# Edge scores of a graph attention layer on one core: a buffer of its own for the 49th bin's rows, a ring of four leaky results, three lane buffers, and the small work of a pair spread over its steps

## The reference, cut to what matters

```python
hij = jnp.concatenate([h[src], h[dst]], axis=-1)
e = jnp.matmul(jax.nn.leaky_relu(jnp.matmul(hij, w), 0.2), a)
exp_e = jnp.exp(e)
denom = jax.ops.segment_sum(exp_e, src, num_segments=N)
```

## Time and profile before

| | us |
|---|---|
| median of 3 runs | 3370.88 |
| lowest and highest run | 3368.73, 3375.42 |
| the profiled execution | 3371.61 |
| its span, first to last instruction | 3369.8 |
| DVE busy in the span | 3095.1 (92%) |
| PE busy / PEld busy | 3073.6 (91%) / 2791.6 (83%) |
| ACT busy | 2725.8 (81%) |

### The profile page before, as it was taken

How to read it: one execution, slowest core, us unless ns; L and a number is a source line. 1 busy time by engine, 2 the same in 40 slices (tenths; PEclk the granted TensorE clock), 3 DMA queues, 4 the chain that set the end, 5 groups by cost and what they waited for, 6 DMA issues and landing times. The chain is left out here.

```text
span 3369.8 us, 100973 instructions
## 1 busy us (share of the span) xinstructions
PE 3073.6 (91%) x39974; PEld 2791.6 (83%) x39974; DVE 3095.1 (92%) x5054; ACT 2725.8 (81%) x6802; POOL 159.1 (5%) x252
## 2 busy tenths in 40 slices
PE   4777689999999999699999999987999999999995
PEld 3666577777777777599999999977999999999994
DVE  7999879998999999899999999978999999999997
ACT  4989777777877777699999999975777777777777
POOL 0000000000000000000000000000111111111110
PEclk9999899999999999799999999998999999999998
DMA  2000022222222222244333333305444445444441
GB/s 63 12 15 12 9 96 90 84 90 85 90 84 85 90 84 72 55 96 96 97 97 97 96 97 97 96 30 182 159 156 156 158 156 158 157 156 158 156 144 40
DMA packets 173164, 333.01 MB, mean 99 GB/s; under 512 B 54849, under 2 KB 108693, under 8 KB 172690
## 3 DMA queue, kind: packets, MB, share of 16 engines
q1 hardware_dynamic: 172690, 326.50, 31.6%
HBM read 320.77 MB, written 5.66 MB: 97 GB/s over the span
## 5 line engine op out<-in xcount | busy, mean ns | idle before, releaser
L942 PE MATMUL l_gathered<-xp,l_src_onehot 128*128 128x128 bf16 x7203 | 466.9, 221 | 11.2 <-DVE l_src_onehot L855 11.2
L647 PE MATMUL sc_z<-sc_onehot,pq 128*128 128x256 f32 (+1 forms) x2450 | 426.5, 296 | 54.5 <-DVE sc_leaky L568 44.9
L1316 PE MATMUL l_gathered<-hp,l_onehot 128*128 128x128 bf16 x7203 | 459.0, 219 | 0.0
L736 ACT ACTIVATE sc_leaky<-sc_z 128x1024 f32<-128x1024 f32 (+3 forms) x325 | 310.1, 954 | 153.0 <-PE sc_z L651 96.3
L942 PEld LDWEIGHTS l_gathered<-xp,l_src_onehot 128*128 128x128 bf16 x7203 | 407.8, 99 | 26.2 <-DVE l_src_onehot L855 11.6
L780 DVE TENSOR_TENSOR l_lane<-iota_b,l_lane_pairs 128x896 bf16<-128x896 bf16 x686 | 421.7, 615 | 0.0
L1330 PE MATMUL l_acc<-e,l_lane_wide 128*128 128x132 f32 x2744 | 399.3, 286 | 16.5 <-ACT e L1385 16.3
L568 DVE SCALAR_TENSOR_TENSOR sc_leaky<-sc_z,sc_leaky 128x1024 f32<-128x1024 f32 (+3 forms) x325 | 369.9, 1138 | 45.6 <-ACT sc_leaky L736 42.2
L1316 PEld LDWEIGHTS l_gathered<-hp,l_onehot 128*128 128x128 bf16 x7203 | 406.7, 98 | 0.4
L651 PE MATMUL sc_z<-sc_onehot,pq 128*128 128x256 f32 (+1 forms) x2450 | 401.0, 286 | 0.0
L647 PEld LDWEIGHTS sc_z<-sc_onehot,pq 128*128 128x128 f32 x2450 | 340.7, 194 | 69.3 <-issue 68.2
(11 more groups left out here) (233 smaller groups left out, 6064.3 us busy)
## 6 DMA issues: line engine op xcount, KB each, us to landing
l_got<-edge_rows_wide SPq DMA_DIRECT2D x343, 448.0 KB, 3.7
l_got<-edge_rows_src SPq DMA_DIRECT2D x343, 224.0 KB, 3.2
placed<-edge_rows SPq DMA_DIRECT2D x144, 512.0 KB, 3.7
out_dram<-X SPq DMA_DIRECT2D x12, 256.0 KB
edge_rows<-bin_bytes SPq DMA_DIRECT2D x98, 6.1 KB
edge_rows_wide<-bin_rows SPq DMA_DIRECT2D x98, 12.2 KB
placed<-edge_rows SPq DMA_DIRECT2D x24, 64.0 KB, 2.8
placed<-edge_rows SPq DMA_DIRECT2D x6, 256.0 KB, 3.6
```

The lines of the kernel that those rows point to most:

```text
L647: nc.tensor.matmul(z[:, b, 0:nw, :], PQ[:, b0 + b, q, 0:C], hot[:, r % HOTS, b, 0, 0:nw, :], start=(b == u and q == 0), stop=False)
L736: nc.scalar.activation(y, z, ACT.Relu, scale=1.0 - ALPHA).then_inc(s["positive"], 1)
L942: ins = nc.tensor.matmul(gps[:, t % 2, i * P:(i + 1) * P], hot[:, t % RING, i, :], parts[:, g * GX + i, q, :], start=(q == 0), stop=(q == 2))
L1316: ins = nc.tensor.matmul(gps[:, t % 2, i * P:(i + 1) * P], dst_hot[:, t % RING, i, :], hp[:, g * GX + i, q, 0:C], start=(q == 0), stop=(q ...
```

## The change

Five things are changed in `score_edges`, and one line outside it.

1. The bytes of the 49th bin go to a tile of their own, `sc_last_rows`, with a semaphore of its own. The two-part buffer now holds the six full groups of a pair alone, so group 0 of a pair waits for group 4 of the pair before, and group 1 for group 5.
2. `sc_leaky` is a ring of four steps, chosen by r modulo 4. `positive(r)` waits for the `dot` of step r-4. The memory is as large as before.
3. There are three lane buffers for two: `lane_hot` waits for the `add` of the item three before.
4. `split3` is gone. Its two casts go to ACT (`take_high`, `take_middle`) and its two subtractions stay on DVE (`take_rest`, `take_low`), each in a round of its own; `keep`, `turn`, `exponent` and `stage` move to other rounds too. A function `slots` holds the rounds.
5. The lane items of a pair begin in round 11 of the next pair and not in round 0 of the one after it, and those of the last pairs are drawn together, two or three to a round, so the loops end after 332 rounds and not 351.

The tile `SL` outside is laid out without its unused rows and columns.

```diff
-    HOTS, EARLY = 3, 3
+    HOTS, EARLY, RING, LANES = 3, 3, 4, 3
...
+        last_got = sb("last_rows", [P, R_BYTES], mybir.dt.uint8)
...
-        zl = sb("leaky", [P, 2, 2, 1024])
+        zl = sb("leaky", [P, RING, 1024])
...
-        ohs = sb("lane_onehot", [P, 2, GX, P], BF16)
+        ohs = sb("lane_onehot", [P, LANES, GX, P], BF16)
...
+        def slots(pair):
+            first = (pair + 1) * PER
+            if pair == PAIRS - 2:
+                at = dict(keep=3, turn=4, exponent=5, stage=5, high=6, rest=6, middle=7, low=7)
+                items = [8 + i // 2 for i in range(DEN)]
+            elif pair == PAIRS - 1:
+                at = dict(keep=2, turn=2, exponent=2, stage=1, high=2, rest=2, middle=2, low=2)
+                items = [2 + i // LANES for i in range(DEN)]
+            else:
+                at = dict(keep=3, turn=4, exponent=6, stage=7, high=7, rest=8, middle=9, low=10)
+                items = [11, 12, 12] + list(range(13, 24)) if pair < PAIRS - 3 else [11 + i // 2 for i in range(DEN)]
+            return {n: first + a for n, a in at.items()}, [first + a for a in items]
...
+        LAST = slots(PAIRS - 1)[1][-1] + 1
...
+                    for j in range(6):
+                        if pair >= 1 or j >= 2:
+                            used = last_group_step(pair, j - 2) if j >= 2 else last_group_step(pair - 1, j + 4)
+                            sp.wait_ge(s["hot"], used + 1)
+                            sp.wait_ge(s["away"], late_steps(used + 1))
+                        load(pair, j, 8, got[:, j % 2], loaded[j % 2])
+                    if pair >= 1:
+                        sp.wait_ge(s["hot"], last_group_step(pair - 1, 6) + 1)
+                    load(pair, 6, 1, last_got[:], last_loaded)
...
-                def split(pair):
...
+                def take_rest(pair):
+                    n0, nw = 2 * pair, (2 if pair < PAIRS - 1 else 1)
+                    dve.wait_ge(s["part_high"], pair + 1)
+                    if pair >= 1:
+                        dve.wait_ge(s["part_middle"], pair)
+                        dve.wait_ge(s["parts"], pair)
+                    nc.vector.tensor_tensor(rest[:, 0:nw], e0[:, n0:n0 + nw, 0:NB], ep[:, pair % 2, 0:nw, :, 0], ALU.subtract
+                                            ).then_inc(s["part_rest"], 1)
+
+                def take_low(pair):
+                    nw = 2 if pair < PAIRS - 1 else 1
+                    dve.wait_ge(s["part_middle"], pair + 1)
+                    nc.vector.tensor_tensor(ep[:, pair % 2, 0:nw, :, 2], rest[:, 0:nw], ep[:, pair % 2, 0:nw, :, 1], ALU.subtract
+                                            ).then_inc(s["parts"], 1)
...
-                    if c >= 2:
-                        dve.wait_ge(s["added"], c - 1)
+                    if c >= LANES:
+                        dve.wait_ge(s["added"], c - LANES + 1)
...
-                for r in range(R + 2 * PER):
-                    pair, step = divmod(r, PER)
+                for r in range(LAST):
...
-                    if step % 2 == 0 and g >= 2:
-                        act.wait_ge(s["dotted"], g - 1)
+                    if r >= RING:
+                        of_pair, of_step = divmod(r - RING, PER)
+                        act.wait_ge(s["dotted"], group_of(of_pair, of_step // 2) + 1)
...
+                def take_high(pair):
+                    n0, nw = 2 * pair, (2 if pair < PAIRS - 1 else 1)
+                    act.wait_ge(s["exp"], pair + 1)
+                    if pair >= 2:
+                        act.wait_ge(s["added"], (pair - 1) * DEN)
+                    nc.scalar.copy(ep[:, pair % 2, 0:nw, :, 0], e0[:, n0:n0 + nw, 0:NB]).then_inc(s["part_high"], 1)
+
+                def take_middle(pair):
+                    nw = 2 if pair < PAIRS - 1 else 1
+                    act.wait_ge(s["part_rest"], pair + 1)
+                    nc.scalar.copy(ep[:, pair % 2, 0:nw, :, 1], rest[:, 0:nw]).then_inc(s["part_middle"], 1)
```

More of the change, by code:

```diff
@@ L86, in link @@
         self.wait(self.mark(ins))
-def split3(nc, chain, value, hi, mid, lo, rest):
-    chain.link(nc.vector.tensor_copy(hi, value))
-    chain.link(nc.vector.tensor_tensor(rest, value, hi, ALU.subtract))
-    chain.link(nc.vector.tensor_copy(mid, rest))
-    return nc.vector.tensor_tensor(lo, rest, mid, ALU.subtract)
 NBK = 49
@@ L623, in _ @@
                         compare_count()
-                    if step == 10 and 1 <= pair <= PAIRS:
-                        split(pair - 1)
-                    if 2 <= pair:
-                        for i in ((step,) if step < PER - 1 else (step, step + 1)):
-                            if i < len(den_items(pair - 2)):
-                                lane_hot(pair - 2, i)
+                    if r == slots(PAIRS - 1)[1][0]:
+                        for i in range(LANES):
+                            lane_hot(PAIRS - 1, i)
+                    for pair in due("rest", r):
+                        take_rest(pair)
+                    for pair in due("low", r):
+                        take_low(pair)
+                    for pair, i in items_due(r):
+                        if pair < PAIRS - 1 or i >= LANES:
+                            lane_hot(pair, i)
                 dve.wait_ge(s["closed"], 1)
@@ L768, in _ @@
                         positive(r - 1)
-                    pair, step = divmod(r, PER)
-                    if step == 5 and pair >= 1:
-                        keep(pair - 1)
-                    if step == 8 and pair >= 1:
-                        exponent(pair - 1)
-                    if step == 11 and pair >= 1:
-                        stage(pair - 1)
+                    for pair in due("keep", r):
+                        keep(pair)
+                    for pair in due("exponent", r):
+                        exponent(pair)
+                    for pair in due("stage", r):
+                        stage(pair)
+                    for pair in due("high", r):
+                        take_high(pair)
+                    for pair in due("middle", r):
+                        take_middle(pair)
 def compare_lanes(nc, k, out, lanes):
```

82 lines of the change are left out of this document (35 added, 47 removed).

## The result

The changed kernel takes 3325.85 us, the median of four runs (3325.31 to 3327.88). The kernel before took 3371.14 us in the same job, also over four (3368.73 to 3375.42). The ratio is 0.9863, with a 95% interval from 0.9848 to 0.9878: faster, by 45 us where I had forecast 37. The profiled execution took 3327.88 us with a span of 3326.1, where that of before had 3371.61 and 3369.8, so the two traces differ by 43.7 us.

A forecast was written before the change was run, and what follows sets the result against it. PE was taken to bound the kernel, pausing at each pair's end. Pairs -29.6, first two pairs -4, end -5.4, last pair +2 make -37 us from 3371.6: 3334.6, so 3334 for a median, range 3320 to 3348 (64%).

The forecast's parts named there:

- PE bounds the pair, and stands still at its end: A pair of 37.56 us is PE's work, 35.16, plus 1.87 of waits and 0.53 of half clock.
- The wait left: PE's wait for `leaky` of step 11 at each pair's end: 0.72 us stay, bounds 0 and 1.2.
- The half clock: Stretches at clock 0.50 behind pairs' ends: half of them stay, 0.27 us a pair, bounds 0 and 0.53.
- PE's work: PE's rounds of a pair without waits, summed from the starts of `gather`: 35.16 us.
- The ends: First two pairs 4 us less, stretch behind the last `leaky` 5.4 less, last pair's rounds 2 more.
- the tail: Behind the last `leaky`, 11 lane items for 21: 8.2 us for 13.6, so 5.4 less.
- Small work: Two casts from DVE to ACT, 0.3 us each there: hidden beside PE's work, room on DVE but no time.
- The spread work becomes the wait: Rival, 17%: both casts on ACT come in full, 14 us, and all half-clock stretches stay, 5.6: 3354 us.
- PE was never full: Rival, 4%: DVE is the true limit, a pair falls to 33.8 us and the kernel to 3285.
- The wait only moves: Rival, 8%: PE's 1.87 us return at other rounds and only the end is shorter: 3368 us.
- Slower: Rival, 7%: `take_middle` misses `take_rest` by a DVE step, 2.60 us a pair, 55 us: 3389 us.

The follow-up runs named there:

- u_split: The changed kernel with the split as four DVE instructions in round 10 again and no casts on ACT: 3333.76 us.
- d_wait: The changed kernel with one more DVE instruction in round 11, a reduction of some 1.0 us whose result nobody reads: 3385.22 us.
- u_rows: The changed kernel with the 49th bin's bytes back in the two-part buffer: 3368.66 us.
- u_ring: The changed kernel with the ring of four undone, `sc_leaky` again in two halves of two steps: 3325.95 us.
- o_lanes: The kernel before with the third lane buffer alone: 3372.95 us.
- u_lanes: The changed kernel with two lane buffers and not three: 3354.47 us.
- o_rows: The kernel before with the own tile for the 49th bin alone (`SL` in its new layout): 3344.81 us.
- o_three: The kernel before with own tile, ring of four and third lane buffer, no work moved (`SL` in its new layout): 3333.53 us.
- m_item: The changed kernel with the lane item of round 11 put into round 14: 3324.86 us.
- d_fill: d_wait with 18 matmuls that add zero put on PE in round 12, where PE would wait: 3350.43 us.

## Why the prediction was right, step by step

**PE bounds the pair, and stands still at its end.** Right. The wait left was worked out at 0.72 us and is 0.70 (16.8 / 24), through the chain in which it was expected. Each lengthening of DVE in rounds 10 and 11 shows there (u_split 0.96, d_wait 1.7), and each lengthening of ACT by a transfer (u_rows 1.5).

**Which part carries it.** The prediction took the three buffers together and asked what is late next. Built up one by one: the tile 26 us (3371 to 3345), the third lane buffer 11 (to 3333.5, with the ring, which by u_ring is worth nothing), the spread of the small work and the earlier items 8 (to 3326). Taken away one by one the tile is worth 43, the third lane buffer 13, the ring 0, the split 8 and the early items 4. They don't add, because the clock does not go with the pauses in proportion: u_rows brings back 14 half-clock stretches where before had eight. In the same way o_lanes takes 9 us of waits from PE while the tile is missing, and gets 15 stretches.

**The half clock** is the term that I mis-sized. I let half of the stretches stay, 0.27 us a pair; none did in the 21 pairs, so 5.6 us more came in. "TensorE: Matmul & The Clock Gate" of the Trainium skill has, in "What's actually happening", activity as what releases the throttle; taken as I took it, that shorter pauses leave no stretch, it would have given that, and over the pairs the trace agrees (0.98 to 1.00). For the last pair of four other kernels it does not, as the last section shows. The row did not carry my half. That only eight of 21 pauses had been followed by a stretch said nothing on pauses of 0.7 us, of which the trace of before had none at a pair's end. And I had misread the trace when I wrote that the stretches stand only behind waits of 1.6 us and more: four of the eight follow pauses of 1.25 to 1.36 us. One of them, on PE and in the windows of before:

```profile
1172.91 0.86 PE L647 MATMUL sc_z<-sc_onehot,pq 128*128 128x256 f32 x4 [1.25 <-DVE sc_leaky L568]
```

```profile
1173.30:1176.70 3.40, 3.40 (x19) 2.94 (x21) 1.79 (x3) 1.23 (x2) 0.00 (x0) 0.50 0.25 94
```

**PE's work.** I had 35.16 us a pair and measured 35.72 - 0.70 = 35.02. The 0.14 are one round: I took round 2 from behind a wait, as 2.60 less 0.26 = 2.34, and it takes 932.76 - 930.58 = 2.18, like every other round with neither `dot` nor `turn`. A wait that a row names need not be all the delay behind it: where that second wait comes or goes (u_lanes, o_rows to o_three) the row names 0.27 or 0.28 us and the pair changes by 0.41. These 3 us and the clock's 5.6 make up the 9 by which the pairs came out better.

**The ends.** The first two pairs gave 5.0 (I had 4), the tail 4.9 (5.4), the last two pairs cost 2.4 (2).

**Small work.** One cast on ACT takes 0.36 and 0.35 us, where I had 0.3, and is hidden as said; its successor starts 0.18 and 0.16 us behind it, so the rival that charged both casts in full had them too dear as well. On DVE the casts were not only room: u_split has them at 0.26 a pair. In the sum this error did not show, because the chain of the prediction let `leaky` of step 10 start as soon as its product was there, without any `split3` ahead of it.

**The rivals.** *The spread work becomes the wait*: false, ACT has no wait at L790 and PE none from round 3 to 11. *PE was never full*: false. Pairs are 35.72 and not 33.8, and PE has 803 of 820 us in matmuls, 98%. The rule of "Perfetto Trace Analysis" of the Trainium skill, in "Identifying the Most-Contended Engine", which judges PE's headroom by MFU (the share of peak flops) and the weight loads, would leave it room by the latter, since they fill only 79% of the stage (650.5 of 820 us); the trace does not agree. *The wait only moves*: false as forecast, but true of the item of round 11 alone (m_item). *Slower*: false, no wait of DVE's step length appeared.

## What to carry to other kernels

Where one engine bounds a loop but pauses once in each turn, find the chain that ends the pause and work out what is late next. Take parts of a change away and also put them in alone: here one part was worth 26 us alone and 43 when taken away, of which the clock was 11 and 21. When work is moved, ask where the bounding engine's pause is: work inside it is free (d_fill's is even a gain), and the same work put elsewhere is not (m_item).
